# Two transformer layers on one core: loads and row maxima of the first pair before attention, the last token tiles and chunks of the experts' stage side by side, the scan's clears on GpSimd

## What is computed

```python
x = layernorm(x + differential_attention(x))   # 16 pairs of heads, causal
x = layernorm(x + experts(x))                  # 8 experts of 64, the best 2, and low-rank parts
x = layernorm(x + mamba2(x))                   # 64 heads of 64, state 128
x = layernorm(x + quantised_ffn(x))            # 512 to 2048 to 512, silu gate
# differential attention, of each pair of heads:
aw = softmax(q @ k.T + causal)                 # for each of the two heads
aw = aw[:, :, 0] - lam * aw[:, :, 1]
lam = exp(sum(lq1 * lk1)) - exp(sum(lq2 * lk2)) + LAMBDA_INIT
```

## Time and profile before

| | us |
|---|---|
| median of 3 runs | 3575.68 (3574.21 to 3576.49) |
| the profiled execution | 3574.93, its span 3572.9 |
| TensorE busy | 3372.2 (94%) |
| VectorE busy | 2682.4 (75%) |
| ScalarE busy | 2108.8 (59%) |
| GpSimd busy | 881.3 (25%) |

### The profile page before, as it was taken

One profiled execution on the slowest core, in us unless ns is written; L12 is line 12 of the kernel. 1 busy time (PEld: TensorE's weight loads), 2 busy tenths in 40 slices (PEclk: granted clock), 3 DMA queues, 4 the chain that ended last, 5 costly groups with the idle time before them and its releaser, 6 DMA issues. The chain is left out here.

```text
span 3572.9 us, 58326 instructions
## 1 busy us (share of the span) xinstructions
PE 3372.2 (94%) x20672; PEld 2379.9 (67%) x20672; DVE 2682.4 (75%) x5220; ACT 2108.8 (59%) x3372; POOL 881.3 (25%) x821
## 2 busy tenths in 40 slices
PE   8889999999999888986999999999999999979998
PEld 6644444444444476765777777777777777758886
DVE  3567777777777484565999989999999899964444
ACT  3146666656666733433777777777777777753332
POOL 0022222222222300001344434443444343420000
PEclk9989999999999998997999999999999999989999
DMA  7433343443442311226666766677666766640100
GB/s 229 77 86 87 103 106 91 107 90 90 108 90 78 121 42 32 86 101 230 230 218 222 261 235 227 223 259 242 231 220 235 249 230 226 220 145 27 36 12 24
DMA packets 264128, 529.34 MB, mean 148 GB/s; under 512 B 32544, under 2 KB 55200, under 8 KB 260768
## 3 DMA queue, kind: packets, MB, share of 16 engines
q1 hardware_dynamic: 263840, 525.62, 46.9%
HBM read 429.55 MB, written 95.42 MB: 147 GB/s over the span
## 5 line engine op out<-in xcount | busy, mean ns | idle before, releaser
L527 ACT ACTIVATE probs<-prob_scores 128x1024 f32<-128x1024 f32 (+3 forms) x640 | 572.5, 896 | 381.5 <-PE prob_scores L457 373.6
L477 PE MATMUL times_v<-probs,VS 128*64 128x256 f32 (+2 forms) x4608 | 612.8, 382 | 15.1 <-ACT outT L561 12.9
L583 DVE TENSOR_REDUCE part_max<-ring 128x1 f32<-128x512 f32 x720 | 463.1, 685 | 115.5 <-PE ring L449 113.8
L49 PE MATMUL sc_pip<-sc_xh,sc_wl 128*128 128x512 f32 x1024 | 456.0, 445 | 26.3 <-DMA sc_xl<-x_low 19.2
L1651 POOL TENSOR_TENSOR sc_xdd<-sc_xdt,sc_small 128x512 f32<-128x512 f32 x128 | 245.6, 1919 | 845.9 <-DVE sc_xdt L1860 845.9
L477 PEld LDWEIGHTS times_v<-probs,VS 128*64 128x64 f32 x4608 | 279.9, 136 | 255.0 <-issue 163.1
L51 PE MATMUL sc_pip<-sc_xh,sc_wh 128*128 128x512 f32 x1024 | 405.0, 396 | 0.0
L50 PE MATMUL sc_pip<-sc_xl,sc_wh 128*128 128x512 f32 x1024 | 403.8, 394 | 0.0
L1785 ACT ACTIVATE sc_M<-sc_later,sc_small 128x128 f32<-128x128 f32 x1024 | 311.8, 390 | 0.0
L1851 DVE SCALAR_TENSOR_TENSOR sc_ca<-sc_xr,sc_chan,sc_ca 128x512 f32<-128x512 f32 x384 | 290.9, 758 | 13.6
L457 PE MATMUL prob_scores<-QS,KS 50*128 50x512 f32 (+3 forms) x1280 | 299.0, 464 | 2.0 <-ACT probs L527 2.0
(11 more groups left out here) (336 smaller groups left out, 7168.0 us busy)
## 6 DMA issues: line engine op xcount, KB each, us to landing
sc_wh<-scan_W_high SPq DMA_DIRECT2D x256, 256.0 KB, 2.8
sc_wl<-scan_W_low SPq DMA_DIRECT2D x256, 256.0 KB, 3.4
sc_later<-scan_acum SPq DMA_DIRECT2D x128, 512.0 KB, 4.8
sc_ce<-scan_expa SPq DMA_DIRECT2D x128, 512.0 KB, 5.2
sc_woh<-scan_Wo_high SPq DMA_DIRECT2D x128, 256.0 KB, 3.9
sc_wol<-scan_Wo_low SPq DMA_DIRECT2D x128, 256.0 KB, 4.8
w_raw<-in_Wg SPq DMA_DIRECT2D x64, 256.0 KB, 2.8
scan_W_high<-w_hi SPq DMA_DIRECT2D x64, 256.0 KB, 2.0
```

The costliest lines, as they stand in the source:

```text
L49: pe.matmul(out, ll, rh, start=start, stop=False)
L477: mm = pe.matmul(po[MV * s:MV * (s + 1), CHUNK - w + n * h:CHUNK - w + (n + 1) * h], VS[p % 2][:, j, :], PT[u % NPT][:, s, n * h:(n + 1) * ...
L527: act.activation(PT[u % NPT][:, :, 0:w], pb[u % 2][:, :, 0:w], ACT.Exp).then_inc(exped, 1)
L583: dve.tensor_reduce(to, slot(n)[:, 0:w], AX.X, ALU.max).then_inc(emptied, 1)
```

## The change

In the projections the load is split in two: load_keys for pair 0 goes into SP's stream behind the 30th output's stores, load_queries before the last output's. The maxima start one V product earlier (SKIP 1) and end at V product 13 (LAST), in 13 groups: twelve of three tiles and a last one of four. The split of the first pair's maxima, their turn and copy and the four row DMAs move from attention's start into this stage, as does lambda (its four loads go before the stores). In attention the seven early tiles of pair 1 go into pair 0's first 33 units, which take 40 tiles instead of 33 (two in units 4, 9, 14, 18, 23, 28 and 32). GpSimd clears VS and stages V first, then sets KS2 and clears mp; the clears of the probability buffers and outT go. In the experts' stage there are 22 slots. Tile 15 is normed in slot 17, and tiles 14 and 15 are turned both in slot 18 (HURRY), tile 15 a slot earlier than before. From slot 18 on, the parts of chunk 2 (M) and chunk 3 (L) lie side by side in hand-written orders, by halves of a part; chunk 3 uses the banks of gate and up. acum and expa are stored with one DMA each, over 64 partitions, in a layout [chunk, head]; the scan reads the same 4 KB rows from it. The scan's state is cleared by GpSimd in two memsets, and sd isn't cleared.

The diff, cut to its core:

```diff
 
...
             at = 64 * s + HD * r
...
-def qkv(nc, g, xT, Wq, Wk, Wv, QD, KD):
...
+def qkv(nc, g, xT, Wq, Wk, Wv, QD, KD, lams):
...
-    SKIP = 2
-    first_tile = [max(n - SKIP, 0) * len(tiles) // (TT - SKIP) for n in range(TT + 1)]
+    SKIP, LAST = 1, TT - 3
+    first_tile = [min(max(n - SKIP, 0), LAST + 1 - SKIP) * len(tiles) // (LAST + 1 - SKIP) for n in range(TT + 1)]
...
+                sp.wait_ge(w_low, 1)
+                for n, v in enumerate(lams):
+                    sp.dma_start(lv[:, n, :], v.partition_broadcast(P)).then_inc(lam_in, 16)
                 for n, (w, m, c) in enumerate(outs):
+                    if n == len(outs) - 1:
+
+                        sp.wait_ge(out[0], 32 * (len(outs) // NS))
+                        sp.wait_ge(prod, len(outs))
+                        load_queries(sp, g.QS[0], QD, 0, loaded[0])
                     sp.wait_ge(low, n + 1)
                     for part, s in enumerate((sh, sl)):
...
+                    if n == K_DONE + 1:
+
+                        sp.wait_ge(out[0], 32 * ((K_DONE - EK) // NS + 1))
+                        sp.wait_ge(ready, 4)
+                        load_keys(sp, g.KS[0], KD, 0, loaded[0])
+                sp.wait_ge(ready, 5)
+                load_keys(sp, g.KS[1], KD, 1, loaded[1])
+                load_queries(sp, g.QS[1], QD, 1, loaded[1])
+                sp.wait_ge(max_copied, 1)
+                sp.wait_ge(loaded[0], 16 * 12)
+                load_max_rows(sp, g.QS[0], mT, max_in)
                 for i in range(NS):
                     sp.wait_ge(out[i], 32 * (len(outs) // NS))
-                sp.wait_ge(ready, 5)
-                sp.wait_ge(prod, len(outs))
-                for b in range(2):
-                    load_pair(sp, g.QS[b], g.KS[b], QD, KD, b, loaded[b])
-                for b in range(2):
-                    sp.wait_ge(loaded[b], 16 * 12)
+                sp.wait_ge(loaded[1], 16 * 12)
+                sp.wait_ge(max_in, 64)
...
+                dve.wait_ge(emptied, 2 * len(tiles))
+                dve.wait_ge(out[0], 32 * (len(outs) // NS))
+                split_row_maxima(dve, nm, mp, g.part, max_all, max_high, max_low, 0)
+                dve.wait_ge(max_turned, 1)
+                dve.tensor_copy(mT, ps[NV][:, 0:P]).then_inc(max_copied, 1)
...
+                    if i == LAST + 1:
+
+                        pe.wait_ge(max_low, 1)
+                        pe.transpose(ps[NV][:, 0:P], mp.bitcast(F32), g.ident[:, :]).then_inc(max_turned, 1)
...
-        q, t = (p + 2, u - START) if u >= START else (p + 1, EARLY + u)
-        return [(q, t)] if q < PAIRS else []
...
-    place = {("turn", 0): 0}
-    for t in range(EARLY):
-        for s in range(2):
-            place["max", 1, t, s] = len(place)
+        if u >= START:
+            of = [(p + 2, u - START)]
+        elif p:
+            of = [(p + 1, EARLY + u)]
+        else:
+
+            of = [(1, t) for t in range(u * NM // START, (u + 1) * NM // START)]
+        return [(q, t) for q, t in of if q < PAIRS]
...
+    place = {}
...
+                def stage_v(p):
+                    pool.tensor_copy(VS[p % 2][:, :, 0:VD], g.V[:, :, p * VD:(p + 1) * VD]).then_inc(v_staged, 1)
+
+                for b in range(2):
+                    pool.memset(VS[b][:, :, :], 0.0).then_inc(setup, 1)
+                pool.wait_ge(setup, 2)
+                for b in range(2):
+                    pool.memset(VS[b][:, :, VD], 1.0).then_inc(setup, 1)
+                stage_v(0)
                 for b in range(2, NQK):
                     pool.memset(KS[b][:, :].bitcast(F32), 1.0).then_inc(setup, 1)
-                for b in range(2):
-                    pool.memset(VS[b][:, :, :], 0.0).then_inc(setup, 1)
...
-                for b in range(NPT):
-                    pool.memset(PT[b][:, :, :], 0.0).then_inc(pt_free, 1)
-                pool.memset(OT[0][:, :], 0.0).then_inc(po_free, 1)
+                pool.memset(mp[:, :].bitcast(F32), 0.0).then_inc(mp_clear, 1)
...
-                sp.wait_ge(setup, NQK - 1)
...
+                sp.wait_ge(setup, 4 + NQK - 2)
...
+                        if p == 0:
+                            pe.wait_ge(setup, 4)
                     if j == 0:
-                        pe.wait_ge(po_free, p * NCH + c + 1)
+                        if p or c:
+                            pe.wait_ge(po_free, p * NCH + c)
...
-                split_maxima(0)
-                copy_maxima(0)
-                for t in range(EARLY):
-                    maxima(1, t)
...
-    SLOTS = TT + LAG + 2
+    SLOTS = TT + LAG - 2
+    HURRY = TT + 2
...
-        bank = lambda c, kind: misc[place(c, kind) % 2]
+        bank = lambda c, kind: (pg, pu)[KIND.index(kind) % 2] if c == NCH - 1 else misc[place(c, kind) % 2]
...
+        def tiles_at(s):
+
+            return [TT - 2, TT - 1] if s == HURRY else [s - 4] if 0 <= s - 4 < TT - 2 else []
+
+        def parts_at(s, order):
+
+            if s >= HURRY:
+                return order[s - HURRY]
             c, part = divmod(s - LAG, QT)
-            return (c, part) if 0 <= c < NCH else (None, None)
+            return [(c, part, half) for half in range(2)] if 0 <= c < NCH else []
+
+        L, M = NCH - 1, NCH - 2
...
+                def store_part(c, part, half):
+                    if (part, half) == (2, 1):
                         for made_by, name, src, out in ((asum_made, "acum", asum, asum_out), (ea_made, "expa", ea, ea_out)):
                             sp.wait_ge(made_by, c + 1)
-                            for grp in range(GROUPS):
-                                sp.dma_start(D[name][grp * TT + QT * c:grp * TT + QT * (c + 1), :].rearrange("c (h l) -> h c l", l=CL),
-                                             src[grp * GH:(grp + 1) * GH, :].rearrange("h (c l) -> h c l", l=CL)).then_inc(out, 16)
-                    if part == 3:
+                            sp.dma_start(D[name][QT * c:QT * (c + 1), :].rearrange("c (h l) -> h c l", l=CL),
+                                         src[:, :].rearrange("h (c l) -> h c l", l=CL)).then_inc(out, 16)
+                    if (part, half) == (3, 0):
...
                         sp.dma_start(D["small"][:, :, QT * c:QT * (c + 1), :, :], sm[:, :, :, :, :]).then_inc(small_out, 16)
+                    if (part, half) == (3, 1):
...
+                        if i % QT == QT - 1:
+                            c = i // QT
...
+                    for of in parts_at(s - 1, (((M, 2, 1), (M, 3, 0)), ((M, 3, 1),), ((L, 2, 1),), ((L, 3, 0), (L, 3, 1)))):
+                        store_part(*of)
...
+                    if c == NCH - 1 and KIND.index(kind) < 2:
+
+                        pe.wait_ge(silu, TT)
+                        pe.wait_ge(mul, TT)
+                    elif n >= 2:
...
+                    for i in tiles_at(s):
+                        turn_x(i)
+                    for of in parts_at(s, (((M, 2, 0), (L, 0, 0), (M, 3, 0)), ((L, 1, 0), (L, 1, 1), (M, 3, 1)), ((L, 2, 0),), ((L, 3, 0), (L, 3, 1)))):
+                        scan_part(*of)
...
+                    for of in parts_at(s, (((M, 2, 0), (L, 0, 0), (M, 2, 1)), ((L, 1, 0), (L, 1, 1), (M, 3, 1)), ((L, 2, 0), (L, 2, 1)), ((L, 3, 1),))):
+                        scan_part(*of)
...
+                    if 0 <= s - 3 < TT - 1:
                         norm(s - 3)
                     if 0 <= s - 2 < TT:
                         add(s - 2)
+                    if s - 2 == TT - 1:
+                        norm(TT - 1)
                     if 0 <= s - 1 < TT:
                         low_gated(s - 1)
-                    if 0 <= s - 4 < TT:
-                        low_x(s - 4)
-                    c, part = at(s)
-                    if c is not None:
-                        scan_part(c, part)
+                    for i in tiles_at(s):
+                        low_x(i)
+                    for of in parts_at(s, (((M, 2, 0), (M, 3, 0)), ((L, 1, 0), (M, 3, 1)), ((L, 2, 0),), ((L, 3, 0), (L, 3, 1)))):
+                        scan_part(*of)
...
+                def by_head(t, name):
+                    return D[name][chunk_of(t), group_of(t) * GH * CL:(group_of(t) + 1) * GH * CL].partition_broadcast(P)
...
+                pool.memset(st[:, 0, :], 0.0).then_inc(cleared, 1)
+                pool.memset(st[:, 1:, :], 0.0).then_inc(cleared, 1)
...
-                for buf in (st[:, :, :], sd[:, :]):
-                    dve.memset(buf, 0.0).then_inc(cleared, 1)
```

More of the change, by code:

```diff
@@ L186, in _ @@
                                              op1=ALU.subtract).then_inc(low, 1)
+                dve.wait_ge(lam_in, 64)
+                for n in range(2):
+                    dve.tensor_tensor(lp[:, n, :], lv[:, 2 * n, :], lv[:, 2 * n + 1, :], ALU.mult).then_inc(lam, 1)
+                dve.wait_ge(lam, 2)
+                for n in range(2):
+                    dve.tensor_reduce(le[:, n:n + 1], lp[:, n, :], AX.X, ALU.add).then_inc(lam_sum, 1)
                 dve.wait_ge(ready, 3)
@@ L342, in attention @@
```

(16 more changed lines are left out.)

189 lines of the change are left out of this document (89 added, 100 removed).

## The result

The changed kernel takes **3555.49 us** (median of 4 runs, 3553.29 to 3559.20) beside 3575.92 of the kernel before on the same chip: ratio 0.9945, 95% interval 0.9929 to 0.9961. I had said 3564.5, range 3558 to 3571: faster, as forecast, but by almost twice as much and outside the range. The profiled execution of after (3559.20, span 3557.2) is its slowest, so the two profiles differ by 15.7 us and the medians by 20.4.

What follows compares the result with a forecast made beforehand. TensorE was taken as the bound over most of attention, with gains at three gaps. Span 3572.9 (3574.93) less 7.1 for the seams and 4.0 for the experts gave 3563.8, plus 0.75 to the median 3564.5; range 3558 to 3571.

Steps and rivals of the forecast that it cites:

- the three gaps: TensorE stands still before the first maxima (12.61 us), at attention's start until 198.11, and before chunk 2's and 3's sums (4.88).
- the doubles do stall: Rival said the opposite for pair 0's double tiles in attention: no stall, 5.5 us less, 3559; chance 0.12.
- L: Start of the maxima in the projections, from 125.41 to 119.3; the rival, loads landing as late as now, 3570.6, chance 0.12.
- chunk 2's lateness: Rival in the experts' stage: chunk 2's late sums pass to the stage's end, losing 2.7 us, 3571.2; chance 0.09.
- the stalls: Rival in attention's pair 0: each of seven stalls at double tiles brings half clock, costing 15 us, 3579; chance 0.05.
- Step 1: Projections, first pair's loads: keys issued behind the 30th output's stores bring the maxima's start from 125.41 to 119.3.
- The bound of 115: Projections: earliest start of the maxima allowed for, if the first pair's loads slip between the stores; 119.3 was expected.
- Steps 2 to 4: Projections' end to attention's start: shorter maxima, split moved earlier, times_v waiting for GpSimd alone; times_v 14.6 us earlier, loads included.
- Step 5: Attention's pair 0: seven double tiles cost 7.8 us in stalls and matmuls, bounds 2.3 and 13; half clock gains 0.3.
- Both seams: Projections' end and attention's start together: 14.6 - 7.8 + 0.3 = 7.1 us gained.
- Step 6: Experts' stage: new order and fewer stores issue the last store at 1614.3, not 1618.24; 4.0 us gained, bounds 6 gained, 2.7 lost.
- Step 7: Scan: clearing its state on GpSimd gains nothing, since VectorE is idle for loads to 1636.40.

## Why the prediction was off

**Direction and mechanisms held**: the three gaps shrink where they were said to, GpSimd alone holds the first times_v, the doubles wait for VectorE, chunk 2's sums come late by their own measure (1574.03, with slot 17 10.2 us earlier, so 2.6 later than in the earlier trace rows) and make it good, and nothing shows of the clear. Of the rivals none came: the doubles do stall, L is earlier, chunk 2's lateness doesn't reach the end, and the stalls don't bring the clock down (1.00 from 182.5 to attention's end in after). The sizes, against means over the profiles that share the part:

- **Step 1 failed**, the largest miss of any step. "I take the queue to work in order. A store of 256 KB is taken at 1.1 us like a load" gave L 6.1 earlier; it is 9.5 earlier (124.8 to 115.3). In the profile after the six keys are in 1.6 us sooner than reckoned, and from there the two stores and the six queries take 5.8 us where the step had 8.6. The 119 GB/s of the earlier trace rows were not the queue's rate but that of sixteen engines on one load of 16 partitions. I had the width as a rival only for the pessimistic side. The bound of 115 "loads slip between the stores" was the value that came. The Trainium skill (SBUF — State Buffer, Door 1: The DMA port swizzle) gives 104 GB/s for partitions 0 to 15 and 189 for 0 to 31, in transfers of 1 MiB. The trace agrees in kind: 119 to 137 here for loads in step, somewhat above, and 173 for the mix of 16 and 32 wide. The same page of the Trainium skill ("Can I just issue two DMAs to hit both halves?") says that two transfers serialize and can't be fused. The 195 GB/s in a window of 16-wide loads behind stores show otherwise, and the measurement decides.
- **Steps 2 to 4**: from L to times_v 9.5 us less (72.8 to 63.3, over the kernels with no tile ahead); I had 8.5. In the first pair of profiles it is 9.0: the maxima took 0.4 more than I had (47.6 us to the last group), the split, its turn and its copy 1.5 instead of 1.9, some 0.3 of that by the cast's 0.18, and times_v stands 4.9 behind the opening instead of 5.2. The other 0.5 of the mean isn't followed up.
- **Step 5**: doubles and clock cost 7.0 us where half clock is short after the opening (6.8 us; 1046.0 to about 1053.0) and 11.4 where it is long (20.5 us; 1057.4), 8.8 in the mean; I had 7.5. The stall of 0.8 was right for five of the seven doubles, and the other two wait less.
- **Both seams** so 10.2 us earlier at attention's end, not 7.1; the run with them alone, 9.9 by the medians.
- **Step 6**: 5.4 instead of 4.0: 2.8 for the order, 2.6 for the stores. In the first pair of profiles the last CB store is 3.3 us earlier once the 10.2 by which slot 17 already stood earlier are taken off, and the scan's first load 4.4. I ended the sum at the last store; that this store itself lands 3.2 us after its issue behind the bunched stores, and 2.0 without them, was left out.
- **Step 7**: nothing to be seen.

So 10.2 + 5.4 = 15.6. That the first two profiles differ by 15.7 is in part chance: between them attention ends 12.8 us earlier, 1.4 is lost again before chunk 0's CB store, the chunks give only 0.6 (at clock 0.89 before and 0.87 after), the stores 2.6 and the scan 1.1.

In the two comparisons of the whole change the medians moved by 20.4 and 18.9 us. The rest, 3 to 5 us, isn't settled. Two stretches in which no step had a gain are a little shorter on average over the kept profiles: from attention's end to chunk 0's CB store 268.1 instead of 269.4 us, and from the scan's first matmul to the end 1943.2 instead of 1944.4. But each spreads by more than that within one arrangement: the first takes 270.9 and 265.6 us in two profiles of the same changed kernel, with the clock ahead of the experts' stage at 0.84 and 0.88, and the second runs from 1939.7 to 1948.8 with no pattern I can name. So this is an observation and not a cause.

The range: the misses of the steps together, 4.5 us (3.4 of them step 1's), would have given 3560, inside it. What took the median below 3558 is that rest, whose cause stays open; I had set the range about one profiled execution of before, without room for what else moves from one execution to the next (3569 to 3584 us for the kernel before over these comparisons).

## What to carry over

A rate read from one kind of transfer in one arrangement is not the queue's rate: ask how many partitions the transfers in flight reach together, and where nothing waits for the wide transfers, put narrow loads behind and among them rather than in a row on an empty queue. When a stage ends in many small stores, count their issue and what they do to the stores behind them: eight stores each for two tensors cost 2.6 us against one each, 1.5 by their issue and 1.1 by the landing of the last store. A gain of 3 us at a seam can vanish in where the half clock falls, so it is to be read from the stretch at like clock, not from the time.

## What was not expected

- The same twelve loads of 128 KB, 16 partitions each, at one address range: every 1.0 us when issued alone, every 0.7 on average behind mixed traffic, with the DMA engines busy for 0.83 of the time instead of all of it.
- Changing only which tensor's load comes next moved a load from 1.11 to 0.98 us.
- The chunks' stretch of the experts' stage has two lengths in either order of the parts, 2.5 us apart in the old and 1.9 in the new, and the longer one goes with the lower granted clock.
- Two profiles of one program, the changed kernel, with attention's first times_v at 178.5 in both: half clock for 6.8 us in one and for 20.5 in the other, and pair 1's turn 4.6 us apart.
